# The PSUM bank at which the decoder's rotation begins, and the last output tile of a two-layer graph network computed and stored by halves

## The chip, the cores and the metric

The kernel is one program on one core of a Trainium2 chip. The time is device microseconds (us) of one execution. The core has a matrix engine (TensorE, PE in the profile, its weight loads PEld), a vector engine (VectorE, DVE), a scalar engine (ScalarE, ACT), GpSimd (POOL), and SyncE (SP), which here issues almost all of the DMA transfers. Matrix products land in PSUM, eight banks of 128 partitions x 512 float32; VectorE and ScalarE read them from there.

## What is computed

Two layers of a graph network over 1250 nodes with 1024 features, 20000 edges:

```python
h = jnp.maximum(_layernorm(x), 0.0)
h = sigmoid(h @ wenc.T + benc)                 # encoder, 500 features
agg = segment_sum((h @ conv)[src] * edge_weight[:, None], dst)
hout = agg + h @ lin.T
x = x + hout @ wdec.T + bdec                   # decoder
h = jnp.maximum(_layernorm(x), 0.0)
# second layer: symmetric normalised sum over edges and self loops
out = segment_sum(norm[:, None] * (h @ W.T + b)[col], row)
x = x + out
```

The edge lists become dense matrices: the weighted adjacency for the first layer and edge counts for the second, so that both gathers are matrix products.

## The kernel before

The nodes are cut into ten tiles of 128 rows (the last has 98), T = 10. One function, `schedule()`, writes out a list of steps in one order, and each engine walks that list and issues its own part of each step, in order; semaphores connect the engines. So each engine's queue is that list, and a wait on an engine holds back everything behind it there.

Precision comes from products in three passes: each operand is a high and a low part, and `product` issues high x high, high x low and low x high, three matmuls (lines 1315, 1316 and 1317), all accumulated in one bank.

The steps that matter here:

- **"sk" and "s".** The aggregation for three column blocks n = 0, 1, 2 of 500, 500 and 250 nodes. Four accumulators ("s", n, f), one for each 128 features f, stay in four banks while ten steps ("sk", n, k) add products of adjacency tiles (`unit`) with `g`. Then ScalarE rounds each accumulator to the high part of `hT` (line 909), and VectorE subtracts to get the low part (line 1184), which frees the bank. While block 2 runs, the decoder's weights `wd` are also split: "cut", high part by ScalarE (line 816), low part by VectorE (line 563).
- **"p".** The decoder, one step for each tile t: two products of 12 matmuls each, 128 x 512, into a bank each; VectorE adds each to the tile of x (line 1218) and then takes layernorm statistics. Tile 0 needs `hT` columns 0 to 127 alone, which come from block n = 0.
- **"z".** The second layer's aggregation, 40 groups of 20 matmuls (line 1331), copied by ScalarE.
- **"o".** The second layer's weight product, by a Winograd-Strassen scheme of 7 half-size products p over 5 pairs of tiles b: 35 groups ("o", p, b) of 12 matmuls of 512 columns (HK = 4 slices of three). Each group needs its left operand, which ScalarE and VectorE prepare a few groups earlier, and its right operand. VectorE scales the bank by `dis_u` and adds it to a half of an x tile (line 1301). Products 5 and 6 share an accumulator for each b (`CHAIN`): group ("o", 6, b) goes on adding to the bank of ("o", 5, b). Both are the last of the products that go to their half-tile (`FINAL`), so each is followed by a store of that half-tile from SP's queue (line 714). ("o", 5, 4) and ("o", 6, 4) belong to the tile with 98 rows, and the latter is the last step of the program; after it SP waits for all stores (line 715).

Banks are given out in turn by `bank_for`. Until the decoder the round is over six banks, 0 to 5 (XBANKS = 6), because banks 6 and 7, `wbank`, collect the adjacency's windows early in the program. From the first "p" the round is over all eight, with a counter of its own. Before a group's first matmul TensorE calls `take`, which waits until the bank's previous group has been read:

```python
def take(g):
    if before_in_bank[g] is not None:
        read_done(pe, before_in_bank[g])
    elif banks_of[g] >= XBANKS:
        pe.wait_ge(stage_ready, NW)
    return bank[banks_of[g]]
```

`stage_ready` reaches NW when the last adjacency window has been copied out of banks 6 and 7, long before the decoder. The four accumulators of block 2 lie in banks 5, 0, 1 and 2, in that order.

Of the kernel before, what the change touches and what calls it, by code (L numbers as in the profile page):

```python
# [17 lines left out]
T = 10  # L18
KD = D // P
KF = 4  # L20
# [54 lines left out]
    ((1, 1), 2, (1, 0)),  # L75
)
NP = len(PRODUCTS)

FINAL = {out: p for p, (_, _, out) in enumerate(PRODUCTS)}
CHAIN = {p: max([q for q in range(p) if PRODUCTS[q][1] == PRODUCTS[p][1]], default=None) for p in range(NP)}  # L80
# [21 lines left out]
def tile_rows(t):  # L102
    return min(P, NODES - P * t)
# [159 lines left out]
def build(nc, x, edge_rows, heads_dst, nat_src, nat_dst, nat_w,  # L263
# [19 lines left out]
    dense = (0, XBANKS)  # L283
    for s in STEPS:
        if s[0] == "p":
            dense = (0, 8)
        if s[0] == "swl":
            bank_for(("s", s[1], s[2]), *dense)
        elif s[0] in ("t", "e", "g", "z", "edges"):
            bank_for(s, *dense)  # L290
        elif s[0] == "o":
            if CHAIN[s[1]] is None:
                bank_for(s, *dense)
            else:

                banks_of[s] = banks_of["o", CHAIN[s[1]], s[2]]
                last[banks_of[s]] = s
        elif s[0] == "p":
            for i in range(2):
                bank_for((*s, i), *dense)  # L300
        if s[0] in ("t", "e", "g", "z", "s", "p", "o", "edges"):
            parts = {"s": KF, "p": 2}.get(s[0])
            for g in [s] if parts is None else [(*s, i) for i in range(parts)]:
                accs[g] = len(accs)

                if s[0] in ("s", "p", "o"):
                    frees[g] = len(frees)
                if s[0] in ("t", "g", "s"):
                    his[g] = len(his)
        elif s[0] == "lo":  # L310
            frees[s[1:]] = len(frees)
# [7 lines left out]
    with ExitStack() as ctx:  # L319
# [254 lines left out]
        def slot_of(i):  # L574

            return (i + 1) % 2

        def left_free(eng, p, b):

            i = nth[p, b] - LEFTS  # L580
            if i >= 0:
                acc_done(eng, ("o", i // NB, i % NB))

        @block.sync
        def _(sp):
# [16 lines left out]
            for s in STEPS:  # L602
# [50 lines left out]
                            bring(j)  # L653
                elif s[0] == "fetch":
                    p = s[1]
                    acc_done(sp, ("o", p - 2, NB - 1))
                    sp.dma_start(both[p % 2][:].bitcast(F32), kept[made[p]]).then_inc(kept_in[p], 16)
                elif s[0] == "raw":
                    n = s[1]
# [6 lines left out]
                elif s[0] == "row":  # L666

                    sp.wait_ge(dis_ready, 1)
                    with nc.allow_non_contiguous_dma("single words"):
                        sp.dma_start(row.rearrange("t p -> p t"), dis[:]).then_inc(row_out, 16)  # L670
                    sp.wait_ge(row_out, 16)
                    sp.dma_start(dis_row[:], row.rearrange("t p -> (t p)").unsqueeze(0).broadcast_to([P, NODESP])).then_inc(row_in, 16)
                elif s[0] == "flip":

                    k = s[1]
                    if k == 0:
                        sp.wait_ge(stage_ready, NW)
                        acc_done(sp, ("g", T - 1))
                        sp.wait_ge(blank, 1)
                    sp.wait_ge(loops_in, k + 1)  # L680
                    sp.dma_start(a2[:, :, P * k:P * (k + 1)], cnt[:, k, :], transpose=True).then_inc(flipped, 16)
                elif s == ("load", "wd"):

                    sp.wait_ge(rows_summed, T)
                    sp.wait_ge(flipped, 16 * T)
                    sp.dma_start(cut_of["wd"][0][:], wdec.rearrange("(k p) f -> p k f", p=P)).then_inc(cut_in["wd"], 16)
                elif s == ("s", NS - 1):
                    sp.wait_ge(wl_used, NS)
                    for t in range(T):
                        if t == 4:  # L690
                            sp.wait_ge(unit_ready, T * NS)
                        if t == T - 1:
                            acc_done(sp, ("s", NS - 1, KF - 1))
                        sp.dma_start(x1[t][0:tile_rows(t), :], rows(x, t)).then_inc(xb_in[t], 16)
                    sp.wait_ge(rows_summed, T)
                    sp.dma_start(b1_bc[:], b1.broadcast_to([P, D])).then_inc(b1_in, 16)
                elif s[0] == "layer1":
                    read_done(sp, ("p", T - 1, 1))
                    sp.wait_ge(rows_summed, T)
                    m = sp.value_load(missed[0:1, 0:1], min_val=0, max_val=1)  # L700
                    with sp.If(m != 0):
                        for b in range(NB):
                            if b:
                                sp.wait_ge(rest_used, b)
                            sp.dma_start(a2_rest[:, :, 0:block_cols(b)], rest[:, :, B * b:B * b + block_cols(b)]).then_inc(rest_in, 16)
                            sp.wait_ge(rest_in, 16 * (b + 1))
                    sp.wait_ge(stage_ready, NW)
                elif s[0] == "o":
                    p, b = s[1:]
                    t, i = PRODUCTS[p][2]  # L710
                    if FINAL[t, i] == p:
                        half = slice(512 * i, 512 * (i + 1))
                        read_done(sp, s)
                        sp.dma_start(rows(out, 2 * b + t)[:, half], x1[2 * b + t][0:tile_rows(2 * b + t), half]).then_inc(out_done, 16)
            sp.wait_ge(out_done, 16 * 2 * T)

        @block.gpsimd
        def _(pool):
# [235 lines left out]
        def _(dve):  # L954
# [35 lines left out]
            for s in STEPS:  # L990
# [300 lines left out]
                elif s[0] == "o":  # L1291
                    p, b = s[1:]
                    t, i = PRODUCTS[p][2]
                    t += 2 * b
                    n = tile_rows(t)
                    acc_done(dve, s)
                    if p:
                        read_done(dve, ("o", p - 1, b))
                    dve.wait_ge(xo_ready, t + 1)
                    xs = x1[t][0:n, 512 * i:512 * (i + 1)]  # L1300
                    v.scalar_tensor_tensor(xs, bank[banks_of[s]][0:n, :], dis_u[0:n, t:t + 1], xs, ALU.mult, ALU.add).then_inc(bank_free, 1)  # L1301

        @block.tensor
        def _(pe):
# [32 lines left out]
            def layer1(parts):  # L1337

                for s in STEPS[STEPS.index(("layer1",)) + 1:]:
# [31 lines left out]
                    elif s[0] == "o":  # L1371
                        p, b = s[1:]
                        slot = nth[p, b] % LEFTS
                        if CHAIN[p] is None:
                            o = take(s)
                        else:
                            o = bank[banks_of[s]]
                            read_done(pe, ("o", CHAIN[p], b))
                        pe.wait_ge(left_ready, nth[p, b] + 1)
                        if p < 2:  # L1380
                            pe.wait_ge(right_ready, HK * (made[p] + 1))
                        else:
                            pe.wait_ge(kept_in[p], 16)
                        for k in range(HK):
                            ins = product(o[:], [left[j][:, slot, k, :] for j in range(2)], [right[p % 2][j][:, k, :] for j in range(2)],
                                          CHAIN[p] is None and k == 0, k == HK - 1)
                        ins.then_inc(acc_ready, 1)

            def idle(n):

# [218 lines left out]
```

## Time and profile before

| | us |
|---|---|
| median of 3 runs | 476.97 |
| lowest and highest | 476.15, 477.29 |
| the profiled execution | 475.59 |
| its span, first to last instruction | 473.8 |
| TensorE busy | 463.2 (98%) |
| VectorE busy | 314.7 (66%) |
| ScalarE busy | 203.4 (43%) |

The profiled execution took 475.59, of which 1.79 lie outside of its span. It is 1.38 under the median of the timed runs and 0.56 under the fastest of them. All rows below are from that one execution.

### The profile page before, as it was taken

To read this page: it belongs to the slowest core of one execution; us is meant where nothing else is said; L and a number is where in the kernel's file an instruction comes from. 1 tells how busy PE (TensorE), PEld (TensorE's weight loads), DVE (VectorE), ACT (ScalarE), POOL (GpSimd) and SP (SyncE) were. 2 spreads that over 40 slices of the span, in tenths; PEclk is the share of its full clock that TensorE was granted. 3 is DMA by queue.
4 is the path that set the end of the run, shared out by engine and by line. 5 is a ranking of instruction groups with operands and counts; after the bars stand their busy time and mean duration, and the time that the engine had idled before them with its cause. 6 is when DMAs were issued, how large, how long until landed. Compare 5 with 4: busy or idle time off the path is not lost.

```text
span 473.8 us, 9229 instructions
## 1 busy us (share of the span) xinstructions
PE 463.2 (98%) x3472; PEld 402.9 (85%) x3472; DVE 314.7 (66%) x606; ACT 203.4 (43%) x408; POOL 35.4 (7%) x36
## 2 busy tenths in 40 slices
PE   6999999999999999999899999999999999999997
PEld 5999999978888888889788887888889988888885
DVE  5989886777857852693558777839351646667642
ACT  6985684655542231232425544547352622222220
POOL 3300000000000000000000000365500000000000
PEclk9999999999999999999999999999999999999999
DMA  8720224392113670439430004261969316545542
GB/s 308 254 80 24 66 74 137 88 347 69 66 67 79 128 244 2 112 109 354 188 113 1 0 2 160 107 254 49 386 233 378 129 26 241 199 178 221 201 173 86
DMA packets 37439, 70.26 MB, mean 148 GB/s; under 512 B 16816, under 2 KB 25274, under 8 KB 35730
## 3 DMA queue, kind: packets, MB, share of 16 engines
q1 hardware_dynamic: 37074, 69.24, 42.1%
q8 instruction: 32, 0.52, 0.5%
q0 software_dynamic: 320, 0.39, 0.4%
q14 instruction: 13, 0.11, 0.1%
HBM read 44.33 MB, written 22.01 MB: 140 GB/s over the span
## 4 chain that ended last, share of the span: by engine, by line
PE 91%; DVE 6%; ACT 1%; DMA 1%; issue 0%; POOL 0%; SPq 0%; DVEq 0%; ACTq 0%; POOLq 0%
PE bank L1315 23%; PE bank L1316 22%; PE bank L1317 22%; PE bank L1331 18%; PE bank L1427 2%; DVE stats L972 2%; PE bank L1429 1%; PE bank L1431 1%; PE bank L1447 1%; DVE we L563 1%; DMA h<-x 1%; DVE wd_lo L563 1%; DVE h0T L1068 0%; ACT wd_hi L816 0%; DVE wc L563 0%
## 5 line engine op out<-in xcount | busy, mean ns | idle before, releaser
L1331 PE MATMUL bank<-a,h_hi 128*128 128x256 f16 (+3 forms) x400 | 85.5, 270 | 0.0
L1331 PE MATMUL bank<-a,h_lo 128*128 128x256 f16 (+3 forms) x400 | 85.5, 269 | 0.0
L1315 PE MATMUL bank<-right,left 128*128 128x512 f32 x140 | 54.5, 390 | 0.0
L1317 PE MATMUL bank<-right,left 128*128 128x512 f32 x140 | 54.5, 389 | 0.0
L1316 PE MATMUL bank<-right,left 128*128 128x512 f32 x140 | 54.5, 389 | 0.0
L1301 DVE SCALAR_TENSOR_TENSOR x<-bank,dis_u,x 128x512 f32<-128x512 f32 (+1 forms) x35 | 26.3, 751 | 38.3 <-PE bank L1317 38.3
L936 ACT CAST left<-zs 128x512 fp32r<-128x512 f32 x35 | 21.8, 625 | 64.0 <-PE bank L1317 64.0
L1315 PE MATMUL bank<-unit,g 128*128 128x500 f32 (+3 forms) x120 | 42.3, 352 | 0.4 <-DVE unit L1174 0.4
L1331 PEld LDWEIGHTS bank<-a,h_hi 128*128 128x128 f16 (+1 forms) x400 | 39.0, 97 | 4.1 <-issue 0.3
L1315 PE MATMUL bank<-h0T,we 128*128 128x256 f32 (+3 forms) x144 | 41.5, 288 | 0.8 <-DVE hT L1075 0.8
L1331 PEld LDWEIGHTS bank<-a,h_lo 128*128 128x128 f16 (+1 forms) x400 | 39.2, 98 | 3.7
L1317 PE MATMUL bank<-unit,g 128*128 128x500 f32 (+3 forms) x120 | 42.3, 352 | 0.0
L1316 PE MATMUL bank<-unit,g 128*128 128x500 f32 (+3 forms) x120 | 42.3, 352 | 0.0
L1316 PE MATMUL bank<-h0T,we 128*128 128x256 f32 (+3 forms) x144 | 40.3, 280 | 0.0
L1317 PE MATMUL bank<-h0T,we 128*128 128x256 f32 (+3 forms) x144 | 40.2, 279 | 0.0
L1174 DVE TENSOR_TENSOR unit<-raw,unit 128x500 fp32r<-128x500 f32 (+1 forms) x30 | 17.3, 591 | 31.1 <-ACT unit L901 31.1
L901 ACT CAST unit<-raw 128x500 fp32r<-128x500 f32 (+1 forms) x30 | 16.1, 557 | 49.8 <-PE bank L1317 47.6
L1315 PE MATMUL bank<-wd_hi,hT 128*128 128x512 f32 (+1 forms) x80 | 31.7, 396 | 1.7 <-DVE hT L1184 1.7
L1289 DVE TENSOR_TENSOR right<-whole,right 128x512 fp32r<-128x512 f32 x28 | 25.2, 966 | 10.2 <-ACT right L943 10.2
L1316 PE MATMUL bank<-wd_lo,hT 128*128 128x512 f32 (+1 forms) x80 | 31.6, 395 | 0.0
L1317 PE MATMUL bank<-wd_hi,hT 128*128 128x512 f32 (+1 forms) x80 | 31.4, 393 | 0.0
L1317 PEld LDWEIGHTS bank<-right,left 128*128 128x128 f32 x140 | 26.3, 188 | 5.5
(152 smaller groups left out, 1091.4 us busy)
## 6 DMA issues: line engine op xcount, KB each, us to landing
right_scratch<-right SPq DMA_DIRECT2D x5, 2048.0 KB, 8.6
right<-right_scratch SPq DMA_DIRECT2D x5, 2048.0 KB, 7.6
whole<-w SPq DMA_DIRECT2D x7, 1024.0 KB, 7.5
adj_scratch<-stage SPq DMA_DIRECT2D x50, 125.0 KB, 1.8
raw<-adj_scratch SPq DMA_DIRECT2D x2, 2500.0 KB, 9.3
h<-x SPq DMA_DIRECT2D x9, 512.0 KB, 6.2
x<-x SPq DMA_DIRECT2D x9, 512.0 KB, 5.3
out<-x SPq DMA_DIRECT2D x18, 256.0 KB
```

The source lines that it names most:

```text
L563: ops.tensor_tensor(parts[1][:, s[2], :], raw_w[:, s[2], :], parts[0][:, s[2], :].bitcast(F32), ALU.subtract).then_inc(cut_ready[s[1]], 1)
L901: nc.scalar.copy(units[0][:, u % UNITS, 0:c].rearrange("p (w d) -> p w d", d=W), raw[:, 0:c // W, k, :]).then_inc(unit_hi, 1)
L936: nc.scalar.copy(left[0][:, nth[p, b] % LEFTS, :, :], side(b, PRODUCTS[p][0])).then_inc(left_hi, 1)
L972: ins = v.bn_stats(stats[0:rows, t % 2, i, :], src[:, 512 * i:512 * (i + 1)])
L1174: v.tensor_tensor(units[1][:, u % UNITS, 0:c].rearrange("p (w d) -> p w d", d=W), raw[:, 0:c // W, k, :], units[0][:, u % UNITS, 0:c].bitc ...
L1289: v.tensor_tensor(right[slot_of(i)][1][:, k, :], whole[slot_of(i)][:, k, :], right[slot_of(i)][0][:, k, :].bitcast(F32), ALU.subtract).the ...
L1301: v.scalar_tensor_tensor(xs, bank[banks_of[s]][0:n, :], dis_u[0:n, t:t + 1], xs, ALU.mult, ALU.add).then_inc(bank_free, 1)
L1315: pe.matmul(o, lhs[0], rhs[0], start=first, stop=False, skip_group_check=True)
L1316: pe.matmul(o, lhs[0], rhs[1], start=False, stop=False, skip_group_check=True)
L1317: return pe.matmul(o, lhs[1], rhs[0], start=False, stop=last, skip_group_check=True)
L1331: ins = pe.matmul(o, h1[i][0:n, k, 128 * f:128 * (f + 1)], moving, start=(k == 0 and part == 0 and i == 0), stop=(k == T - 1 and part == p ...
L1427: pe.matmul(o, o_src[:, r, i, :], o_key[:, r, i, 0:2, :], start=(i == 0), stop=False, skip_group_check=True)
```

## The change

Two edits. First, at the first "p" step the counter of the eight-bank round is set to XBANKS, so that the round begins at banks 6 and 7; every later group of "p", "z" and "o" is then two banks behind where it was (modulo 8). Second, the groups ("o", 5, 4) and ("o", 6, 4) are each done in two column halves of 256, in two banks: 12 matmuls of 256 columns for the first half and 12 for the second, a VectorE sum for each half, and a store for each half.

```diff
+HALVED = [("o", NP - 2, NB - 1), ("o", NP - 1, NB - 1)]
...
         if s[0] == "p":
+
+            if dense != (0, 8):
+                turns[0, 8] = XBANKS
             dense = (0, 8)
...
+        def halves(s):
+
+            if s in HALVED:
+                return [((*s, i), slice(256 * i, 256 * (i + 1))) for i in range(2)]
+            return [(s, slice(0, 512))]
...
                     if FINAL[t, i] == p:
-                        half = slice(512 * i, 512 * (i + 1))
-                        read_done(sp, s)
-                        sp.dma_start(rows(out, 2 * b + t)[:, half], x1[2 * b + t][0:tile_rows(2 * b + t), half]).then_inc(out_done, 16)
-            sp.wait_ge(out_done, 16 * 2 * T)
+                        for g, c in halves(s):
+                            cols = slice(512 * i + c.start, 512 * i + c.stop)
+                            read_done(sp, g)
+                            sp.dma_start(rows(out, 2 * b + t)[:, cols], x1[2 * b + t][0:tile_rows(2 * b + t), cols]).then_inc(out_done, 16)
+            sp.wait_ge(out_done, 16 * (2 * T + len(HALVED)))
...
-                    acc_done(dve, s)
                     if p:
-                        read_done(dve, ("o", p - 1, b))
+                        read_done(dve, halves(("o", p - 1, b))[-1][0])
                     dve.wait_ge(xo_ready, t + 1)
-                    xs = x1[t][0:n, 512 * i:512 * (i + 1)]
-                    v.scalar_tensor_tensor(xs, bank[banks_of[s]][0:n, :], dis_u[0:n, t:t + 1], xs, ALU.mult, ALU.add).then_inc(bank_free, 1)
+                    for g, c in halves(s):
+                        acc_done(dve, g)
+                        xs = x1[t][0:n, 512 * i + c.start:512 * i + c.stop]
+                        v.scalar_tensor_tensor(xs, bank[banks_of[g]][0:n, 0:c.stop - c.start], dis_u[0:n, t:t + 1], xs,
+                                               ALU.mult, ALU.add).then_inc(bank_free, 1)
...
-                        for k in range(HK):
-                            ins = product(o[:], [left[j][:, slot, k, :] for j in range(2)], [right[p % 2][j][:, k, :] for j in range(2)],
-                                          CHAIN[p] is None and k == 0, k == HK - 1)
-                        ins.then_inc(acc_ready, 1)
+                        for g, c in halves(s):
+                            if CHAIN[p] is None:
+                                o = take(g)
+                            else:
+                                o = bank[banks_of[g]]
+                                read_done(pe, ("o", CHAIN[p], *g[2:]))
+                            for k in range(HK):
+                                ins = product(o[:, 0:c.stop - c.start], [left[j][:, slot, k, :] for j in range(2)],
+                                              [right[p % 2][j][:, k, c] for j in range(2)], CHAIN[p] is None and k == 0, k == HK - 1)
+                            ins.then_inc(acc_ready, 1)
```

TensorE's queue where the decoder begins. `unit` and `g` belong to the last "sk" step; `wd` and `hT` to ("p", 0), with its waits on its first matmul. Before:

```order
L1315 MATMUL bank2<-unit0_121,g0_117 116x250
L1316 MATMUL bank2<-unit1_122,g0_117 116x250
L1317 MATMUL bank2<-unit0_121,g1_118 116x250
L1315 MATMUL bank0<-wd_hi_149,hT0_85 128x512 [waits wd_ready,bank_free]
L1316 MATMUL bank0<-wd_lo_150,hT0_85 128x512
```

And with the change:

```order
L1330 MATMUL bank2<-unit0_121,g0_117 116x250
L1331 MATMUL bank2<-unit1_122,g0_117 116x250
L1332 MATMUL bank2<-unit0_121,g1_118 116x250
L1330 MATMUL bank6<-wd_hi_149,hT0_85 128x512 [waits wd_ready,bank_free,stage_ready]
L1331 MATMUL bank6<-wd_lo_150,hT0_85 128x512
```

The order of instructions is the same; the target moved from bank 0 to bank 6. The wait on `bank_free` that remains is for block 0 of the aggregation, and the one for bank 0's reader now stands at ("p", 1).

VectorE's queue at the end of the program, the last sums. Before:

```order
L1301 SCALAR_TENSOR_TENSOR x1_7_158<-bank1,dis_u_73,x1_7_158 128x512 [waits xo_ready,bank_free,acc_ready]
L1301 SCALAR_TENSOR_TENSOR x1_9_160<-bank2,dis_u_73,x1_9_160 98x512 [waits xo_ready,bank_free,acc_ready]
L319 UNCONDITIONAL_BRANCH
```

And with the change:

```order
L1315 SCALAR_TENSOR_TENSOR x1_7_158<-bank7,dis_u_73,x1_7_158 128x512 [waits acc_ready,xo_ready,bank_free]
L1315 SCALAR_TENSOR_TENSOR x1_9_160<-bank0,dis_u_73,x1_9_160 98x256 [waits acc_ready,xo_ready,bank_free]
L1315 SCALAR_TENSOR_TENSOR x1_9_160<-bank1,dis_u_73,x1_9_160 98x256 [waits acc_ready]
L325 UNCONDITIONAL_BRANCH
```

One sum of 512 columns became two of 256, the first of which waits for the first half's matmuls alone.

## Rows read from the trace of the kernel before

**Rows 1.** The page: share of engines, then granted clock in 40 slices.

```profile
PE 463.2 (98%) x3472; PEld 402.9 (85%) x3472; DVE 314.7 (66%) x606; ACT 203.4 (43%) x408; POOL 35.4 (7%) x36
...
PEclk9999999999999999999999999999999999999999
```

**Rows 2.** Chain that ended last, shares of the span by engine.

```profile
PE 91%; DVE 6%; ACT 1%; DMA 1%; issue 0%; POOL 0%; SPq 0%; DVEq 0%; ACTq 0%; POOLq 0%
```

**Rows 3.** All waits of TensorE: who it waited for, total us, times, longest.

```profile
PE bank L1392 <- POOL minus_half L733: 2.3, 1, 2.3
PE bank L1315 <- DVE hT L1184: 1.7, 1, 1.7
PE bank L1447 <- ACT h L803: 1.6, 1, 1.6
PE bank L1315 <- DVE hT L1075: 0.8, 1, 0.8
PE bank L1315 <- DVE unit L1174: 0.4, 1, 0.4
```

**Rows 4.** Busy us in stretches: PE, PEld, DVE, ACT, POOL, clock, DMA share, GB/s.

```profile
231.60:233.60 2.00, 0.26 (x3) 0.06 (x1) 2.00 (x5) 0.85 (x4) 0.00 (x0) 1.00 0.94 377
233.60:470.00 236.40, 236.40 (x1460) 201.08 (x1460) 143.87 (x226) 86.17 (x143) 25.00 (x11) 1.00 0.44 162
```

**Rows 5.** Timeline where the decoder begins: start, duration, instruction.

```profile
230.47 2.36 DVE L563 TENSOR_TENSOR wd_lo<-wd_raw,wd_hi 128x1024 fp32r<-128x1024 f32 x2 [0.53 <-ACT wd_hi L816]
...
231.40 0.28 PE L1316 MATMUL bank<-unit,g 98*116 98x250 f32 x1
...
231.52 0.28 PE L1317 MATMUL bank<-unit,g 98*116 98x250 f32 x1
232.75 1.39 DVE L1184 TENSOR_TENSOR hT<-bank,hT 128x250 fp32r<-128x250 f32 x4
...
233.54 0.51 PE L1315 MATMUL bank<-wd_hi,hT 128*128 128x512 f32 x1 [1.74 <-DVE hT L1184]
...
233.88 0.40 PE L1316 MATMUL bank<-wd_lo,hT 128*128 128x512 f32 x1
...
234.12 0.39 PE L1317 MATMUL bank<-wd_hi,hT 128*128 128x512 f32 x1
...
236.70 0.69 DVE L1218 TENSOR_TENSOR x<-bank,x 128x512 f32<-128x512 f32 x1 [2.57 <-PE bank L1317]
```

**Rows 6.** Line 563, `wd` alone: durations in ns, first and last start.

```profile
L563 DVE TENSOR_TENSOR wd_lo<-wd_raw,wd_hi x4: 1221/1226/1226, 224.3 to 231.6; 128x1024 fp32r<-128x1024 f32 x4
```

**Rows 7.** SP's queue at the same place, and that load's median time to landing.

```profile
217.25 15.50 SPq L694 DMA_DIRECT2D x<-x  x10
...
x<-x SPq DMA_DIRECT2D x9, 512.0 KB, 5.3
```

**Rows 8.** Timeline at the end of the program.

```profile
457.42 0.39 PE L1316 MATMUL bank<-right,left 128*128 128x512 f32 x1
...
469.88 0.39 PE L1317 MATMUL bank<-right,left 128*128 128x512 f32 x1
470.31 0.75 DVE L1301 SCALAR_TENSOR_TENSOR x<-bank,dis_u,x 98x512 f32<-98x512 f32 x1 [1.97 <-PE bank L1317]
471.09 0.35 SPq L714 DMA_DIRECT2D out<-x  x1
```

**Rows 9.** Timeline of TensorE in the encoder, ten steps from one to the other.

```profile
39.77 0.28 PE L1316 MATMUL bank<-h0T,we 128*128 128x256 f32 x1
...
40.96 0.27 PE L1317 MATMUL bank<-h0T,we 128*128 128x256 f32 x1
```

**Rows 10.** VectorE's groups by shape: count, busy us, mean ns.

```profile
L1301 DVE SCALAR_TENSOR_TENSOR x<-bank,dis_u,x 98x512 f32<-98x512 f32 x4 | 3.0, 751 | 5.3 <-PE bank L1317 5.3
L1184 DVE TENSOR_TENSOR hT<-bank,hT 128x500 fp32r<-128x500 f32 x6 | 3.9, 675 | 3.2 <-ACT hT L909 3.2
L1184 DVE TENSOR_TENSOR hT<-bank,hT 128x250 fp32r<-128x250 f32 x3 | 1.1, 411 | 0.0
L1034 DVE SCALAR_TENSOR_TENSOR er<-er,er 125x256 f32<-125x256 f32 x1 | 0.4, 426 | 0.0
```

**Rows 11.** What SP's last wait was for, and the landing of a small store.

```profile
SPq L319 <- DMA out<-x: 1.9, 1, 1.9
...
adj_scratch<-stage SPq DMA_DIRECT2D x50, 125.0 KB, 1.8
```

**Rows 12.** Stretches around the last store, and around a lone store of `stage`.

```profile
471.80:473.00 1.20, 0.00 (x0) 0.00 (x0) 0.00 (x0) 0.00 (x0) 0.00 (x0) 1.00 0.54 167
142.20:142.80 0.60, 0.60 (x4) 0.48 (x3) 0.38 (x1) 0.60 (x3) 0.00 (x0) 1.00 0.62 213
```

More of the change, by code:

```diff
@@ L291, in build @@
         elif s[0] == "o":
[L292 to L297, printed above, removed]
+            for g in [(*s, i) for i in range(2)] if s in HALVED else [s]:
+                if CHAIN[s[1]] is None:
+                    bank_for(g, *dense)
+                else:
+                    banks_of[g] = banks_of["o", CHAIN[s[1]], *g[2:]]
+                    last[banks_of[g]] = g
         elif s[0] == "p":
@@ L301, in build @@
         if s[0] in ("t", "e", "g", "z", "s", "p", "o", "edges"):
-            parts = {"s": KF, "p": 2}.get(s[0])
+            parts = 2 if s in HALVED else {"s": KF, "p": 2}.get(s[0])
             for g in [s] if parts is None else [(*s, i) for i in range(parts)]:
@@ L581, in left_free @@
             if i >= 0:
-                acc_done(eng, ("o", i // NB, i % NB))
+                acc_done(eng, halves(("o", i // NB, i % NB))[-1][0])
         @block.sync
@@ L655, in _ @@
                     p = s[1]
-                    acc_done(sp, ("o", p - 2, NB - 1))
+                    acc_done(sp, halves(("o", p - 2, NB - 1))[-1][0])
                     sp.dma_start(both[p % 2][:].bitcast(F32), kept[made[p]]).then_inc(kept_in[p], 16)
@@ L1373, in layer1 @@
                         slot = nth[p, b] % LEFTS
[L1374 to L1378, printed above, removed]
                         pe.wait_ge(left_ready, nth[p, b] + 1)
@@ L1383, in layer1 @@
                             pe.wait_ge(kept_in[p], 16)
-                        for k in range(HK):
-                            ins = product(o[:], [left[j][:, slot, k, :] for j in range(2)], [right[p % 2][j][:, k, :] for j in range(2)],
-                                          CHAIN[p] is None and k == 0, k == HK - 1)
-                        ins.then_inc(acc_ready, 1)
+                        for g, c in halves(s):
+                            if CHAIN[p] is None:
+                                o = take(g)
+                            else:
+                                o = bank[banks_of[g]]
[4 more added lines that the diff above has]
+                            ins.then_inc(acc_ready, 1)
             def idle(n):
```

## The prediction, made before the changed kernel had run

> **What bounds the kernel now.** I read the page first. TensorE is busy for 463.2 us of a span of 473.8, with its granted clock in the top step of every slice, which is the 2.4 GHz level [rows 1], and it makes up 91% of the chain that ended last [rows 2]. So the kernel is a stream of matmuls, and time can be won in three ways alone: fewer or cheaper matmuls, less of TensorE standing idle, or a shorter end after its last matmul. Next I read the list of TensorE's waits, which is complete in five rows [rows 3]: 6.8 us in all, and one of the five is the wait for VectorE's line 1184, 1.7 us, once. The stretches then say that from 233.6 to 470.0 TensorE has no gap: busy for 236.40 of 236.40 us [rows 4]. Hence what moves TensorE's work at 233.6 moves everything after it by the same amount, as long as nothing in there is tied to a fixed time and becomes late. Last I read the timeline at the two places that the change touches, the start of the decoder [rows 5] and the end [rows 8].
>
> **First edit: the decoder's first banks.** The last matmul of the aggregation starts at 231.52, and its predecessor at 231.40, so the steps there are 0.12 apart and TensorE would be ready for the next at 231.64. The decoder's first matmul starts at 233.54 [rows 5]. What it waits for is bank 0, which held the second accumulator of block 2: VectorE's subtraction for it is the second of the four of line 1184, which begin at 232.75 and take 1.39 together. They begin that late because VectorE is busy until about 232.8 with the last two low parts of `wd` [rows 5]. With the change the first product of tile 0 goes to bank 6 and the second to bank 7, whose last readers finished long ago. So the start moves from 233.54 to 231.64: 1.90 us. There is a small addition: the first matmul after the wait takes 0.34 to the next one (233.54 to 233.88), where the next step takes 0.24 (233.88 to 234.12); with no stop before it that 0.10 should go too. Together 2.00. The lower bound is the wait as the profile books it, 1.7, if the restart's extra stays.
>
> Is something else late next? The group needs four slices of `wd`, one for each three matmuls. The last low part starts at 231.6 and takes 1.226 [rows 6], so it ends at 232.83. TensorE wants the fourth slice nine steps of 0.23 after 231.64, at 233.7, so there are 0.9 us to spare; the third slice is ready by 231.7 and wanted at 233.0. The bank that now waits for line 1184 is the one of tile 1: wanted two groups, 24 steps of 0.23 or 5.6 us, after 231.64, at 237.2, while VectorE's four subtractions end at 234.14 [rows 5]. `hT` for tile 0 comes from block 0. VectorE's first sum of the decoder moves from 236.70 to about 234.7, and it is free from 234.14. The tile of x that it adds was issued at 217.25 or a little after, and such a load lands in 5.3 us [rows 7]. The loads of later tiles are issued until 232.75, which is 2.0 us nearer to their use than before, but the tile of the last load is wanted some 50 us later. Everything else in the decoder and behind it hangs from TensorE through semaphores and so moves along with it. The other bank numbers are a rotation of the same round of eight, and each group still follows the same group in its bank as before, except in the last product, where it is one further on; each of those was read several groups of 2.7 us earlier. I cost the rotation at nothing, and if the cover were gone the price would be one such wait.
>
> **Second edit: the matmuls of the two halved groups.** From 457.42 to 469.88 there are 55 steps of TensorE with 512 columns [rows 8], 0.2265 each. Float32 matmuls of 256 columns stand in the encoder: ten steps from 39.77 to 40.96, 0.119 each [rows 9]. A halved group has 24 of these (2.856) for 12 of those (2.718), so it costs 0.138 more, and two of them cost **0.28**. The weight load for each is repeated too; it is under the same pitch, since the encoder's rows have one load for each matmul. The Trainium skill's page "TensorE: Matmul & The Clock Gate", section "Back-to-back issue gap", gives N/2.4 + 2.5 ns for a lone matmul at full clock; by it a step of 512 is 216 ns and two of 256 are 218, so that both groups would cost 0.06 more and not 0.28. The rows differ from it at both widths (226 and 119), and I go by them.
>
> **The last sum.** Now 0.75 us, from 470.31 [rows 8], 751 ns for 98 x 512 [rows 10]. The trace has no such sum of 256 columns from PSUM. A subtraction from PSUM takes 675 ns at 500 columns and 411 at 250 [rows 10], 1.06 ns a column; 751 less 256 of these is 480. From below, the nearest is a SCALAR_TENSOR_TENSOR of 256 columns with no PSUM operand, 426 ns [rows 10]; from above, 751 if width did nothing. I take 480, because the slope is from the same kind of source: **-0.27**. The first half's sum lies under the second half's matmuls (0.48 against 12 x 0.119 = 1.43). In ("o", 5, 4) the two sums make VectorE 0.2 busier, and the next left operand waits behind them; VectorE is busy for 144 of 236 us here [rows 4], and stood idle for 1.97 before its last sum [rows 8], so that is hidden.
>
> **The last store.** Its issue row starts at 471.09 and ends at 471.44 [rows 8]; SP then waits 1.9 [rows 11], so it lands at 473.34, 2.25 after the issue began. The DMA engines work on it for 0.54 of 1.20 us, 0.65 us each [rows 12], for 98 rows of 2 KB. The new last store has 98 rows of 1 KB. The nearest row is the store of `stage`, 128 rows of 1000 bytes: engines at work 0.62 of 0.60, 0.37 us, and landing 1.8 after issue in the median [rows 11, 12]. By that row the last store is 2.25 - 1.8 = **0.45** shorter. Bounds: nothing, if what counts is a fixed latency; 0.5 at most, as 98 rows are fewer than 128. The first half's store is issued 1.43 us earlier, 12 steps of 0.119, and its work of about 0.3 us is done before the second's begins; its issue of 0.35 on SP is over too. The Trainium skill, page "DMA: Bandwidth & Descriptors", section "Anatomy of one DMA", fits 2.0 us + bytes/436e3; by that fit, estimated, 200,704 bytes take 2.46 and 100,352 take 2.23, a gain of 0.23 where I take 0.45.
>
> **The sum.** -2.00 + 0.28 - 0.27 - 0.45 = -2.44. The span goes from 473.8 to 471.4, the profiled execution from 475.59 to 473.15. The median of the runs is 1.38 above the profiled execution, so I put the gain on the median: 476.97 - 2.44 = **474.5**, 0.51% faster. With all lower bounds (1.7 gained, 0.28 lost, nothing from sum and store) the gain is 1.4, and with all upper (2.0, 0.28, 0.33 and 0.5) 2.55.
>
> **Rivals.**
>
> (a) The first edit works and the second one brings nothing or costs: the store's latency stays at 2.25, or the second half's store is slowed by the first's. The end is then 0.28 - 0.27 = 0.0 to 0.28 worse, and the gain 1.7 to 2.0: 475.0 to 475.3. For it: the gap between the last row of work and the landing is a large part of the 2.25. Against it: the row of `stage` [rows 11].
>
> (b) The stall moves within the decoder's start and isn't removed. For it: VectorE and ScalarE are both loaded between 231.6 and 233.6, and the DMA engines too, at 0.94 [rows 4]; if the last low part of `wd` came at 234.5 or later, TensorE would stop at the fourth slice for 0.8 or more. Against it: nothing in the change delays VectorE, and there are 0.9 us to spare. The gain would be 0.3 to 1.3: 475.7 to 476.7.
>
> (c) Slower: TensorE runs without the rest of 1.9 us that it has now from 5 us to the end but for short waits, and its clock is brought down to the 1.2 GHz level somewhere behind it. At that level a step of 0.23 would take about twice as long, so a stretch of 4 us at the lower level would eat the gain, and one of 5.5 us make it 1.4 slower, 478.4. Against it: TensorE is busy for 236 us on end with the clock at 1.00 [rows 4]. It decides from 4 us on.
>
> (d) The change doesn't do what it says, and the wait stays since another condition of the same matmul ended with it: the profile books a wait with several conditions to the last. The other conditions are the first slice of `wd`, whose low part starts at 224.3 [rows 6], the read of block 0, and the windows' copies; all long over. This gives 476.5 to 477.
>
> **How the numbers follow.** My forecast, both edits as worked out with a gain of 2.0 to 2.6: 0.64. (a): 0.20. (b): 0.08. (c): 0.03. (d): 0.02. What is left, 0.03, is for a measured median that lies off by more than the runs of before spread (476.15 to 477.29). No change is what lies within 0.3% or 1.4 us, about what a measurement of this kernel can tell. Forecast and (a) lie beyond 1.4 us, but (a) by 0.3 to 0.6 only, so a fourth of it may be measured as no change; most of (b) and (d) is no change. Faster 0.83, same 0.13, slower 0.04. The range reaches over forecast and (a) and by half of the runs' spread to either side: 473.4 to 476.1.
>
> **What the profile would show.** The wait for line 1184 gone from TensorE's list, the first matmul with `wd` at about 231.6, and 0.23 to its successor; the last low part of `wd` still at 231.6; first sum of the decoder at 234.7; no new wait of TensorE behind it. At the end: 48 matmuls of 128x256 at 0.119, a last sum of 0.48, its store landing 1.8 after issue. The last matmul should start about 1.6 us earlier than now (2.00 - 0.28, less 0.11 for its own shorter step), at 468.3. The prediction is wrong if TensorE waits anew in the first group of the decoder, if the granted clock leaves 1.00, or if the halves' steps are longer than 0.119, as a weight load of 0.19 for each might make them.

## The result and the profile after

| | before | after |
|---|---|---|
| median of 6 runs each, us | 477.11 | 473.31 |
| lowest and highest | 475.61, 477.39 | 472.93, 474.02 |
| the profiled execution | 475.59 | 473.33 |
| its span | 473.8 | 471.5 |

The ratio is 0.9934, with a 95% interval of 0.9918 to 0.995: faster by 0.66%. The medians are 3.8 us apart, where the forecast was 2.4; the two profiled executions are 2.3 apart. Applied to the median of 476.97 from which the forecast was made, the ratio gives 473.8, inside the stated 473.4 to 476.1; the new median itself, 473.31, is a tenth below the lower end. The absolute figure depends on the runs of before that it is held against, which is taken up below. So there are two questions: do the terms of the sum hold, and where do the other 1.4 us come from?

The waits of TensorE in the changed kernel, the whole list (who waited for whom, total us, times, longest). Its lines are shifted by some 13 to 16 against those of before: 1184 is now 1197, 1301 is 1315 and 1315 is 1330.

```profile
PE bank L1408 <- POOL minus_half L746: 2.3, 1, 2.3
PE bank L1330 <- DVE hT L1088: 0.6, 1, 0.6
PE bank L1330 <- DVE unit L1187: 0.4, 1, 0.4
```

The wait for the subtraction of `hT` is gone and none took its place behind it; against [rows 3] the wait for ScalarE's `h` in the opening is also missing, which is not the change's doing: the profile of the unchanged kernel in the first experiment lacks it too.

The timeline where the decoder begins, of TensorE and VectorE in the changed kernel:

```profile
231.77 0.28 PE L1332 MATMUL bank<-unit,g 98*116 98x250 f32 x1
231.89 0.40 PE L1330 MATMUL bank<-wd_hi,hT 128*128 128x512 f32 x1
232.12 0.39 PE L1331 MATMUL bank<-wd_lo,hT 128*128 128x512 f32 x1
...
231.85 1.22 DVE L569 TENSOR_TENSOR wd_lo<-wd_raw,wd_hi 128x1024 fp32r<-128x1024 f32 x1
232.99 1.39 DVE L1197 TENSOR_TENSOR hT<-bank,hT 128x250 fp32r<-128x250 f32 x4
234.94 0.69 DVE L1231 TENSOR_TENSOR x<-bank,x 128x512 f32<-128x512 f32 x1 [0.56 <-PE bank L1332]
```

The decoder's first matmul starts 0.12 behind the aggregation's last, where it was 2.02 [rows 5], and its successor 0.23 later, not 0.34. From the aggregation's last matmul to the decoder's second it is 0.35 now and was 2.36: 2.01 less, against 2.00 forecast. VectorE's four subtractions still run at 232.99, now under the decoder.

The stretch from there to the end (busy us of PE, PEld, DVE, ACT, POOL, then clock, DMA share, GB/s), and the timeline of the end:

```profile
231.60:468.00 236.40, 236.40 (x1483) 201.99 (x1483) 145.82 (x232) 87.23 (x148) 24.98 (x11) 1.00 0.44 165
```

```profile
468.44 0.28 PE L1331 MATMUL bank<-right,left 128*128 128x256 f32 x1
...
468.56 0.28 PE L1332 MATMUL bank<-right,left 128*128 128x256 f32 x1
468.88 0.48 DVE L1315 SCALAR_TENSOR_TENSOR x<-bank,dis_u,x 98x256 f32<-98x256 f32 x1 [0.85 <-PE bank L1332]
469.39 0.34 SPq L727 DMA_DIRECT2D out<-x  x1
```

SP's last wait, from its list of waits:

```profile
SPq L325 <- DMA out<-x: 1.4, 1, 1.4
```

TensorE has no gap from the decoder on. Against [rows 8, 11], the last sum takes 0.48 (was 0.75) and SP waits 1.4 for the last store (was 1.9).

Counted from the aggregation's last matmul the program took 473.8 - 231.52 = 242.3 before and takes 471.5 - 231.77 = 239.7 now: 2.55 less. The opening of this execution was 0.25 later, so the spans differ by 2.3 alone. The terms are thus in order, and the 1.4 us of the medians lie in something that the two profiled executions don't show.

### The profile page after: what moved, and what is told of

Its sections match the earlier page's. It is cut to its first block, busy times and chain, and to the rows that moved or that the text cites. A ratio compares the mean times of both kernels' runs of the same rounds, so it can differ in the third digit from the quotient of the medians.

```text
span 471.5 us, 9281 instructions
## 1 busy us (share of the span) xinstructions
PE 465.3 (99%) x3496; PEld 405.8 (86%) x3496; DVE 314.1 (67%) x608; ACT 203.2 (43%) x408; POOL 35.3 (7%) x36
## 4 chain that ended last, share of the span: by engine, by line
PE 92%; DVE 5%; DMA 1%; ACT 1%; issue 0%; POOL 0%; SPq 0%; DVEq 0%; ACTq 0%; POOLq 0%
PE bank L1330 23%; PE bank L1331 22%; PE bank L1332 22%; PE bank L1346 18%; PE bank L1443 2%; DVE stats L985 2%; PE bank L1445 1%; PE bank L1447 1%; PE bank L1463 1%; DVE we L569 1%; DMA h<-x 1%; DVE h0T L1081 0%; DVE wc L569 0%; DVE wd_lo L569 0%; ACT wd_hi L829 0%
## 5 line engine op out<-in xcount | busy, mean ns | idle before, releaser
L1330 PE MATMUL bank<-right,left 128*128 128x512 f32 (+1 forms) x148 | 56.0, 378 | 0.0
L1331 PE MATMUL bank<-right,left 128*128 128x512 f32 (+1 forms) x148 | 55.9, 378 | 0.0
L1332 PE MATMUL bank<-right,left 128*128 128x512 f32 (+1 forms) x148 | 55.9, 378 | 0.0
L1315 DVE SCALAR_TENSOR_TENSOR x<-bank,dis_u,x 128x512 f32<-128x512 f32 (+2 forms) x37 | 26.7, 722 | 38.7 <-PE bank L1332 38.5
L1330 PEld LDWEIGHTS bank<-right,left 128*128 128x128 f32 x148 | 27.8, 188 | 5.2
L1332 PEld LDWEIGHTS bank<-right,left 128*128 128x128 f32 x148 | 27.8, 188 | 5.2
L1331 PEld LDWEIGHTS bank<-right,left 128*128 128x128 f32 x148 | 27.8, 188 | 5.1
L1330 PE MATMUL bank<-wd_hi,hT 128*128 128x512 f32 (+1 forms) x80 | 31.6, 395 | 0.0
```

The costliest lines, as they stand in the source:

```text
L1315: v.scalar_tensor_tensor(xs, bank[banks_of[g]][0:n, 0:c.stop - c.start], dis_u[0:n, t:t + 1], xs, ALU.mult, ALU.add).then_inc(bank_free, 1)
L1330: pe.matmul(o, lhs[0], rhs[0], start=first, stop=False, skip_group_check=True)
L1331: pe.matmul(o, lhs[0], rhs[1], start=False, stop=False, skip_group_check=True)
L1332: return pe.matmul(o, lhs[1], rhs[0], start=False, stop=last, skip_group_check=True)
```

## The experiments

The single runs of before suggested what: 475.61, 476.15, 476.97, 477.24, 477.29 and 477.39. The first four experiments ran together on one chip, and only the expectation of the first of them uses letters, with this meaning: theory A, the missing 1.4 us are scatter that comes through the opening; rival B, every undisturbed run of before takes 477.2. Their results led to another pair, which all later expectations mean. **Theory A**: the runs of before are two clusters; in the upper one TensorE's granted clock falls to its lower level (1.2 GHz) for a while behind the stop at 231.6, so the stop costs some 1.7 us more than its length. **Rival B**: the upper cluster comes from the opening alone.

### The kernel before against itself

> The kernel before, unchanged, timed against itself. The traces explain about 2.5 us of the 3.8 by which the medians moved. Theory A (the rest is how the executions of one kernel scatter, through the opening of the program): ratio 1.000 within 0.3%, and its single runs spread over 475.6 to 477.4, with the granted clock not the same in all. Rival B (every undisturbed run of before takes 477.2, and the profiled one at 475.6 was a rarity): the runs cluster at 477.2 within 0.3 us.

Edit: none. Measured: median 475.68 in 12 runs, with 477.23 for the same program in the 23 runs beside it; ratio 0.9987 (0.997 to 1.0005). All 35 runs together show the two clusters and nothing between: 19 at 475.5 to 476.0, 16 at 477.1 to 478.3. None of the 16 had a mean granted clock above 0.996, while 14 of the 19 lower ones had 1.0. The other five lower ones had 0.996 as well, as the profiled execution of before has, so the mean clock of a run doesn't tell its cluster. So a median of this kernel says which cluster held the majority, and can move by 1.5 us with no change at all. Of the expectation, A's ratio held and the clocks do differ, but the runs lie in two groups and reach 478.3; B, that nearly all are at 477.2, is wrong. Whether the opening makes the groups, these runs don't say.

### The first edit alone

```diff
-HALVED = [("o", NP - 2, NB - 1), ("o", NP - 1, NB - 1)]
+HALVED = []
```

> First edit alone: the round of eight banks begins at bank 6, the last group whole. By the prediction's terms: 2.0 us less than before, wait for the subtraction of hT gone, no new wait of TensorE, end of the program as before. Rival (rotation of all later banks brings something of its own, or the opening changed): 3.4 us less.

Measured: 473.86 median of 6, five at 473.67 to 473.95 and one at 475.17; ratio 0.9938 (0.9918 to 0.9957). Against the median of before's lower cluster (475.64) that is 1.8 less, against that of its upper one (477.4) 3.5. Both figures named in the expectation, 2.0 and 3.4, come out nearly, one for each cluster, and this edit has the whole unexplained part. Of the 0.2 missing from the 2.0, the trace shows 0.09 at the end: VectorE's last sum starts 0.52 behind the last matmul (468.97 to 469.49), where it was 0.43 in before [rows 8]. All kernels with the last groups whole that were made from the changed kernel have this 0.52 or 0.53; why is not shown.

The run at 475.17 is the profiled one, and it shows what a late opening is. The first row is its wait for ScalarE's `h`, the others are its stretches (busy us of PE and so on, then the clock):

```profile
PE bank L1463 <- ACT h L816: 1.7, 1, 1.7
```

```profile
7.00:12.00 5.00, 3.27 (x35) 2.91 (x35) 3.80 (x14) 2.23 (x2) 2.11 (x2) 0.82 1.03 406
12.00:18.00 6.00, 6.00 (x34) 5.24 (x33) 5.97 (x13) 6.00 (x13) 4.47 (x5) 0.58 1.02 334
```

TensorE stopped for 1.7 us at about 10 and then worked at the lower level until 17.0 (0.58 over these 6 us is 0.50 for 5 of them); its last aggregation matmul started at 232.62 instead of 231.4 to 231.9 as in the other traces. That is worth up to 1.1 us. SP's last wait was 2.3 in this execution instead of 1.9, another 0.4.

The same place shows directly that the clock falls at a stop of this length in some executions and not in others. These are the 16 matmuls behind the wait for `h`, and the stretch from 11.0 to 13.5, first in the trace of before, then in that of the kernel whose round begins at bank 3 (below):

```profile
11.04 3.30 PE L1447 MATMUL bank<-ident,h 128*128 128x128 f32 x16 [1.55 <-ACT h L803]
11.00:13.50 2.50, 2.46 (x12) 2.46 (x13) 2.43 (x7) 2.50 (x4) 2.15 (x3) 0.50 1.06 406
```

```profile
11.19 2.23 PE L1463 MATMUL bank<-ident,h 128*128 128x128 f32 x16 [1.67 <-ACT h L816]
11.00:13.50 2.50, 2.27 (x19) 2.01 (x20) 2.43 (x7) 2.50 (x5) 2.15 (x3) 1.00 1.06 406
```

Seven of the kept traces have this wait, of 1.3 to 1.7 us. In five of them (both profiles of before that have it, each edit alone, the start at bank 2) the clock fell to 0.50 before the wait was over, in two (the starts at banks 3 and 5) it stayed at 1.00. In before the low stretch, from 10.4 to 13.8, cost nothing that can be seen: the aggregation's last matmul starts at 231.52, as in executions without it. The clock column isn't complete, though: in the first experiment's profile of before it says 1.00 throughout, yet the twelve matmuls of line 1392 that start at 8.90 take 2.66 us there, where in the execution of [rows 1] they need 1.44. So a mean of 1.00 doesn't prove full speed in the opening.

### The second edit alone

```diff
-                turns[0, 8] = XBANKS
+                turns[0, 8] = 0
```

> Second edit alone: the round begins at bank 0 as before, the last groups by halves. By the terms: +0.28 of TensorE, -0.27 of the last sum, -0.45 of the last store, 0.44 us less in all, the wait of 1.7 at the decoder still there. Rival (the halves carry the unexplained part): 1.8 us less.

Measured: 476.65 median of 12; ratio 0.9993 (0.9976 to 1.001), no difference that can be measured. But the clusters can be read apart: five runs at 474.94 to 475.41, median 475.11, which is 0.5 below before's lower cluster, and seven at 476.54 to 477.65, median 476.85, 0.5 below its upper one. The edit brings the forecast half a microsecond and leaves the two clusters in place.

### Both edits again

Edit: none against the changed kernel.

> Both edits, the changed kernel again on this chip: the sum of the two before, 2.44 us less by the terms; 3.8 if the first comparison of medians stands.

Measured: 473.2 median of 6 (473.0 to 474.11); ratio 0.9931 (0.991 to 0.9952). Its four lower runs, 473.0 to 473.28, are 2.5 under before's lower cluster; the other two are 0.9 and 1.0 above them.

### The stop filled with useless matmuls

In the kernel before, ahead of the decoder's first group, with FILL = 7:

```diff
+                    if t == 0:
+                        cut_done(pe, "wd", 0)
+                        pe.wait_ge(stage_ready, NW)
+                        for i in range(FILL):
+                            pe.matmul(bank[7][:, :], st[0][:, 0, 0:P], wd[0][:, 0, 0:512], start=True, stop=True, skip_group_check=True)
```

> The kernel before plus seven extra matmuls of 512 columns into bank 7, whose result nobody reads, between the aggregation's last matmul and the decoder's first: TensorE works through the stall instead of standing idle, and the stall itself stays. Single runs of before stand in two clusters, 475.5 to 476.0 and 477.1 to 478.3, the upper one never with a mean granted clock of 1.000. Theory A (in about half of the executions TensorE's granted clock falls to the lower level behind the stall and costs 1.7 more): no run in the upper cluster, all at 475.5 to 476.0, but for up to 1.0 more from the opening; the ratio to before 0.998. Rival B (the upper cluster comes from the opening alone): half of the runs at 477.1 or above, ratio 1.000. The seven fill 1.6 of 1.74 us, so that neither theory has them delay the decoder.

Measured: all 12 runs at 475.45 to 475.96, while 21 of 29 of the kernel before beside it were at 476.97 or more (the rest at 475.47 to 475.69); ratio 0.9977 (0.9966 to 0.9988). The timeline of TensorE:

```profile
231.54 0.28 PE L1318 MATMUL bank<-unit,g 98*116 98x250 f32 x1
231.66 1.78 PE L1559 MATMUL bank<-wd_hi,hT 128*128 128x512 f32 x7
233.55 0.51 PE L1316 MATMUL bank<-wd_hi,hT 128*128 128x512 f32 x1
```

The decoder starts at 233.55 as before (233.54), still kept by bank 0's reader. All that changed is that TensorE had work meanwhile, and the upper cluster vanished. This decides against B: work that produces nothing, placed at 231.66, removes it. Two of the 12 runs have a mean clock of 0.991, so it was low somewhere in them; they took 475.93 and 475.96, 0.4 more than the others at most. Luck is unlikely: if only a fourth of the executions belonged to the upper cluster, 12 lower ones in a row would come in 3 of 100 cases.

### Stops of other lengths

The first edit alone, with the round beginning at bank 5, and in two more kernels at 2 and at 3:

```diff
-                turns[0, 8] = XBANKS
+                turns[0, 8] = 5
```

> The round begins at bank 5, whose reader is the first of the four subtractions. The stall falls to about 1.4: lower cluster 475.3 on both theories. A: fewer runs above than before. B: the same share.

> The round of eight begins at bank 2, whose reader is the last of the four subtractions; the last group whole. The stall grows from 1.74 to about 2.4. Lower cluster 476.3 on both theories. A: more than half of the runs 1.7 above it, at 478.0. B: the same share of upper runs as before.

> The round begins at bank 3; banks 3 and 4 held accumulators of block 1 that were read long before. If the gain of the first edit is that the first decoder groups get banks without a pending reader, and nothing particular to banks 6 and 7: no stall, the same as with the start at bank 6, 473.8 (2.0 less than before's lower cluster). If the rotation by two itself did something: another time.

The wait in each profile, for the starts at 5 and at 2:

```profile
PE bank L1330 <- DVE hT L1197: 1.4, 1, 1.4
```

```profile
PE bank L1330 <- DVE hT L1197: 2.4, 1, 2.4
```

| round begins at | stop, us | runs | lower cluster | runs in the upper cluster |
|---|---|---|---|---|
| bank 5 | 1.4 | 12 | 475.33 | 3 |
| bank 0 (before, the 29 runs beside) | 1.7 | 29 | 475.61 | 21 |
| bank 2 | 2.4 | 12 | 476.43 | 6 |
| bank 3 | none | 6 | 473.85 | 0 |

The lower clusters are where the stops put them, within 0.2. The start at bank 3 (ratio 0.9938, 0.9921 to 0.9955) does what the start at bank 6 does (473.86), so the gain is a bank without a pending reader and no property of banks 6 and 7. The share of upper runs does not grow steadily with the length: theory A's guess of more than half at 2.4 us gave just half, fewer than at 1.7 (ratio 1.0009, 0.9993 to 1.0024, for the start at 2; 0.9977, 0.9961 to 0.9992, for the start at 5).

### A long stop

On top of the start at bank 2, in VectorE's part of the last subtraction:

```diff
+                        for i in range(7 if (n, f) == (NS - 1, KF - 1) else 0):
+                            link(v.tensor_tensor(st[1][0:m, f, S * n:S * n + c], bank[banks_of[g]][0:m, 0:c],
+                                                 st[0][0:m, f, S * n:S * n + c].bitcast(F32), ALU.subtract))
```

> As the kernel with the start at bank 2 (stall 2.4, lower cluster at 476.4), but VectorE repeats the last of the four subtractions seven times before the one that frees the bank, some 0.45 us each, so the stall is about 5.6 us. The stall alone gives 476.4 + 3.2 = 479.6. Theory A (a stop at this place lets the granted clock fall for a while behind it, at a cost of 1.7): most or all runs at 481.3, and the profile shows a clock of 0.5 for some us from about 233 on, with TensorE's steps of 0.23 at 0.45 there. Rival B: the runs spread as those of before, over 479.6 and 481.3 half and half, and the clock in the profile falls in the opening alone.

Measured: 481.21, 481.44, 482.27 and 482.51; ratio 1.011 (1.0081 to 1.014). No run at 479.6. TensorE's timeline and the stretches around the stop:

```profile
231.75 0.28 PE L1335 MATMUL bank<-unit,g 98*116 98x250 f32 x1
237.59 0.79 PE L1333 MATMUL bank<-wd_hi,hT 128*128 128x512 f32 x1 [5.56 <-DVE hT L1200]
238.18 0.63 PE L1334 MATMUL bank<-wd_lo,hT 128*128 128x512 f32 x1
238.61 0.63 PE L1335 MATMUL bank<-wd_hi,hT 128*128 128x512 f32 x1
```

```profile
235.00:237.00 2.00, 0.00 (x0) 0.00 (x0) 1.86 (x5) 0.00 (x0) 0.00 (x0) 0.97 1.03 418
...
239.00:241.00 2.00, 2.00 (x6) 1.58 (x5) 0.00 (x0) 0.00 (x0) 0.00 (x0) 0.50 0.95 274
...
243.00:245.00 2.00, 2.00 (x9) 1.60 (x8) 0.69 (x1) 0.00 (x0) 0.00 (x0) 0.83 0.00 0
245.00:247.00 2.00, 2.00 (x11) 1.60 (x10) 0.72 (x2) 0.00 (x0) 0.00 (x0) 1.00 0.00 0
```

Here the fall at this place is seen directly, though behind a stop three times as long as that of before. The granted clock is 1.00 as the stop begins, falls to 0.50 shortly before it ends, and TensorE's steps are 0.43 instead of 0.23 until about 243.7. Against the profile with the 2.4 us stop the decoder starts 3.19 later counted from the aggregation's end, but the program ends 5.99 later: 2.8 us were lost to the clock in this execution, more than the 1.7 expected.

### The kernel before, profiled once more

> The kernel before, unchanged, one more profiled execution, to catch one of the upper cluster (about half of them). If it comes at 477.1 or more: theory A expects the granted clock at 0.5 for a stretch that begins shortly behind the stall (233.5), 3.4 us long, and the aggregation's last matmul at the usual 231.5; rival B expects the aggregation's last matmul at about 233.2 and no low clock behind the stall. If it comes at 475.6 it tells nothing.

Edit: none. It came at 475.63, in the lower cluster, and so doesn't decide; its one low stretch is that in the opening. No profiled execution of before lies in the upper one.

### The last sum and store by halves, the product whole

On top of the first edit (the second one left out), for the last group alone:

```diff
+                    if s == LAST:
+                        for i2 in range(2):
+                            hc = slice(256 * i2, 256 * (i2 + 1))
+                            v.scalar_tensor_tensor(xs[:, hc], bank[banks_of[s]][0:n, hc], dis_u[0:n, t:t + 1], xs[:, hc],
+                                                   ALU.mult, ALU.add).then_inc(last_sums, 1)
...
```

and in SP's part two stores, each behind its own sum.

> First edit, and of the second one only the sum and the store of the last group by halves: its matmuls stay at 512 columns in one bank. By the terms: no cost on TensorE, the second half's sum ends 0.96 after the product instead of 0.75, the last store is 0.45 to 0.5 shorter: 0.25 less than the first edit alone, so 473.6 where that had 473.85 in its lower cluster, and 0.3 more than both edits. If a store of half the size landed no sooner, 474.05.

Measured: 473.52 median of 6 (473.28 to 473.69); ratio 0.9939 (0.9918 to 0.996). That is 0.3 less than the first edit alone and 0.3 more than both, near what the terms say, with SP's last wait again at 1.4. So the half-size store does land about 0.5 sooner, shown here without the halved matmuls. Those runs are of another chip; the start at bank 3 (473.85), which does the same as the first edit, ran on this one and gives the same 0.3. Of this, 0.09 is the start of the last sum: this kernel was made from before, and its sum starts 0.43 behind the last matmul. So I take the 0.3 as right in size and no more.

### The cut at column 320

```diff
-                return [((*s, i), slice(256 * i, 256 * (i + 1))) for i in range(2)]
+                return [((*s, i), slice((0, CUT)[i], (CUT, 512)[i])) for i in range(2)]
```

with CUT at 320.

> Both edits, but the last groups cut at column 320 instead of 256, so that the last part has 192 columns. By the terms: TensorE's 12 steps of 320 and 12 of 192 take 12 x (0.147 + 0.092) = 2.87 a group if the pitch goes on falling with the columns, as for two of 256 (2.86); the last sum is 0.07 shorter (1.06 ns a column), the last store at most 0.1: 0.1 to 0.2 less than both edits at 256, 473.0. If the weight load of 0.19 holds the pitch up below 256 columns, the steps of 192 stay at 0.119 and a group costs 0.33 more: 473.7.

Measured: 473.79 median of 7 (473.46 to 474.32); ratio 0.9943 (0.9922 to 0.9965). It is about 0.5 slower than the cut at 256, on two chips. TensorE's timeline, the second and the twelfth step of the last group's 192 columns:

```profile
467.71 0.28 PE L1332 MATMUL bank<-right,left 128*128 128x192 f32 x1
...
468.83 0.28 PE L1333 MATMUL bank<-right,left 128*128 128x192 f32 x1
```

Ten steps in 1.12: 0.112 each, where 0.092 was wanted and 256 columns take 0.119. The steps hardly get shorter below 256 columns; a group costs 12 x (0.147 + 0.112) = 3.11 instead of 2.86. The hopeful branch of the expectation fell, and the second, with the step held up, came close. Nor did the still smaller last store land sooner: SP's last wait was 1.6 here and 1.4 with 256 columns. Of all kernels run, the one with both edits as given is the fastest.

## Why the prediction was right, and where its size was off

**The stop.** Its removal was forecast at 2.00 and measured 2.01 between the traces, of which 0.11 is the slower restart. The reasons given for nothing being late next held: the last low part of `wd` ended at 233.07 (231.85 and 1.22), wanted at 234.0; the first sum of the decoder at 234.94, counted from the aggregation's end 0.01 from the forecast. With the wait gone from the list and no new one in the decoder, rivals (b) and (d) fell.

**The matmuls.** From the decoder's second matmul to the program's last it was 236.00 [rows 5, 8] and is 236.44. Of these 0.44, 0.11 were expected since the last step is itself shorter and so starts later, and 0.28 as the cost of the halves; 0.05 is over. The steps of 256 columns are 0.119 or 0.12, as in the encoder [rows 9]. The cost, 0.33 with the part that is over, is far from the 0.06 that the prediction worked out from the formula on the Trainium skill's page "TensorE: Matmul & The Clock Gate", section "Back-to-back issue gap".

**Sum and store.** The last sum takes 0.48 as read from the slope [rows 10]. From the store's issue to the end of the span it was 2.7 and is 2.1; 0.45 was forecast, 0.6 came, of which SP's wait has 0.5. Rival (a), nothing from the second edit, fell with it. The 0.23 that the prediction set beside its 0.45, from the fit on the Trainium skill's page "DMA: Bandwidth & Descriptors", section "Anatomy of one DMA", was too small by half; that section gives the fit for transfers that GpSimd issues, and SP issues this one. All four terms add to 2.55 in the traces against 2.44 forecast.

**What was missed** is the step on the median: "The median of the runs is 1.38 above the profiled execution, so I put the gain on the median". It took the 1.38 for an offset that both kernels share. It was the difference between two clusters of before, and the upper one depends on the very stop that the change removes. Of the 77 runs of the unchanged kernel in the experiments (35, 29, 12 and 1), 41 lie in the upper cluster, about 1.6 us above the lower one (477.2 or 477.4 against 475.6); of the 37 runs of kernels without the stop, one lies 1.3 above its kernel's lower runs, which is the late opening and longer last wait shown above, five lie 0.6 to 1.0 above, and none lies further. Half of 1.6 is the mean worth, and all of it shows in a median that falls in the upper cluster: 2.4 + 1.4 = 3.8. That the ratio came out inside the range is in part luck: the forecast's own baseline, 476.97, was a median from the upper cluster, and nothing in the sum accounts for the cluster's part of the gain.

**Rival (c)** had the clock in it, and the wrong way round: it had TensorE's clock brought down for want of a rest. The runs show that the rest is what brings it down, and steady work keeps it up: with the stop filled, 0 of 12. Its sum was off, too: time spent at half speed loses half of its length, so 4 us at the lower level cost 2.0 and don't eat 2.44, and 5.5 us leave the kernel 0.3 slower, not 1.4. And a case of it stood in the trace that the prediction read: "its granted clock in the top step of every slice" is true of slices of 11.8 us, which hide the 0.50 from 10.4 to 13.8. The Trainium skill's page "TensorE: Matmul & The Clock Gate", section "HAM oscillation — how this bites in real kernels", tells of a clock that falls while TensorE waits for data between groups, in waits of 3 to 5 us. The profile with 5.6 us agrees. Here much shorter stops came with a fall in a part of the executions: 1.3 to 1.7 us in the opening, seen in five traces of seven, and 1.4 to 2.4 us at the decoder, inferred from the clusters.

**What stays open.** That the upper cluster is a fall of the clock behind the stop of 1.7 us at 231.6 is inferred: from the mean clock of the upper runs, never above 0.996; from the fill; from the long stop's profile; and from the falls at the stop in the opening. No trace of an upper execution of before was caught. Why one execution falls and the next doesn't, and why the share was 3 of 12, 21 of 29 and 6 of 12 at 1.4, 1.7 and 2.4 us, isn't settled. Shares of 12 runs say little here: the unchanged kernel itself had 3 of 12, 13 of 23, 21 of 29 and 4 of 12.

## What to carry to other kernels

When single runs of one program form two clusters, read them apart before comparing medians, and ask what in the program could decide between them: here a stop of 1.7 us of an otherwise full TensorE cost 2.0 us always and 1.6 more in about half of the executions. Removing such a stop is worth more than its length in the trace. A stop that can't be removed can be filled with matmuls that nobody reads, as long as they end before it does; that alone gave 0.23%. When accumulators are read late, give the next stage banks that have no pending reader, and at the very end of a program halve the last output only as far as the matmul's step still shrinks with its width.

## What was not expected of the hardware

- The clock's fall behind a short stop: seen in five of seven traces at 1.3 to 1.7 us of standing idle in the opening; at the decoder, inferred, 1.6 us for a stop of 1.7 in about half of the executions, and, seen, 2.8 us in one with a stop of 5.6.
- A float32 matmul's step with a weight load each: 0.2265 us at 512 columns, 0.147 at 320 (466.01 to 467.48 is ten steps in that profile), 0.119 at 256, 0.112 at 192. From 512 to 256 it halves nearly; below that it hardly falls.
- A store of 98 rows of 1 KB is confirmed 0.5 us sooner than one of 98 rows of 2 KB (SP's wait 1.4 against 1.9). The DMA engines' work on it fell from 0.65 us each [rows 12] to 0.40, by this stretch of the changed kernel, 0.40 of 1.00 us:

```profile
470.20:471.20 1.00, 0.00 (x0) 0.00 (x0) 0.00 (x0) 0.00 (x0) 0.00 (x0) 1.00 0.40 117
```
